# Attention weighing over a pair of units on eight 64x32 tiles, probabilities turned in place, six score buffers, tables laid out anew

## Time and profile before

| what | value |
|---|---|
| median of 3 runs | 2744.55 us |
| the runs | 2733.57, 2748.24, 2744.55 us |
| span of the profiled execution (first to last instruction) | 2740.3 us |
| TensorE busy, mean granted clock | 2332.0 us (85%), 0.951 of full speed |
| VectorE, ScalarE, GpSimd busy | 2165.5 (79%), 1538.2 (56%), 1436.9 us (52%) |
| image 5, from its norm0 to that of image 6 | 310.4 us |
| from the end of the last convolution to the end | 210.6 us |

### The profile page before, as it was taken

How to read it: one execution, slowest core, us unless ns; L and a number is a source line. 1 busy time by engine, 2 the same in 40 slices (tenths; PEclk the granted TensorE clock), 3 DMA queues, 4 the chain that set the end, 5 groups by cost and what they waited for, 6 DMA issues and landing times.

```text
span 2740.3 us, 67622 instructions
## 1 busy us (share of the span) xinstructions
PE 2332.0 (85%) x27766; PEld 1395.9 (51%) x27766; DVE 2165.5 (79%) x3697; ACT 1538.2 (56%) x3566; POOL 1436.9 (52%) x1150
## 2 busy tenths in 40 slices
PE   0457738899899989899898989899898999899887
PEld 0433326455654556554664556555664556545454
DVE  6877957878887798878887798869887788867655
ACT  1222126654775566754775566754766567655665
POOL 3324562456734574465834575465834575465455
PEclk9878969999999999999999999999999989999999
DMA  5400400115111331115111241105110241101121
GB/s 155 127 3 16 158 19 18 32 47 171 33 33 47 98 105 33 33 35 174 40 33 39 83 128 33 32 32 161 57 33 25 79 146 33 33 32 57 54 63 41
DMA packets 125428, 176.20 MB, mean 64 GB/s; under 512 B 72496, under 2 KB 114240, under 8 KB 115520
## 3 DMA queue, kind: packets, MB, share of 16 engines
q1 hardware_dynamic: 125120, 171.88, 20.0%
HBM read 98.95 MB, written 72.86 MB: 63 GB/s over the span
## 4 chain that ended last, share of the span: by engine, by line
PE 54%; DVE 23%; ACT 8%; issue 6%; POOL 4%; DMA 2%; SPq 2%; DVEq 0%; POOLq 0%; ACTq 0%
PE F L2082 18%; PE QP L2141 9%; PE QP L2148 4%; PE SP L2173 4%; PE F L1979 3%; PE O L2201 3%; PE QP L2157 3%; PE PTR L2183 2%; PE F L1955 2%; DVE g_raw L1423 2%; DVE xs L1836 2%; DVE mx L1847 1%; ACT xs L1201 1%; POOL tmp L960 1%; DVE sums L1855 1%
## 5 line engine op out<-in xcount | busy, mean ns | idle before, releaser
L2082 PE MATMUL F<-g_raw,cw_hi 128*128 128x512 f16 x2304 | 701.1, 386 | 20.7 <-DVE g_raw L1423 6.5
L1201 ACT ACTIVATE xs<-xs,mx 128x64 f32<-128x64 f32 x1792 | 445.7, 334 | 123.8 <-DVE mx L1847 123.8
L915 POOL TENSOR_TENSOR xs<-xs,rec 128x512 f32<-128x512 f32 x256 | 287.9, 1136 | 432.5 <-DVE rec L1857 428.3
L2082 PE MATMUL F<-g_raw,cw_lo 128*128 128x512 f16 x1152 | 443.8, 385 | 0.0
L2082 PEld LDWEIGHTS F<-g_raw,cw_hi 128*128 128x128 f16 x2304 | 224.2, 99 | 286.5 <-issue 17.8
L1208 ACT ACTIVATE prt<-PTR 128x512 f32<-128x512 f32 x256 | 151.0, 590 | 216.8 <-PE PTR L2183 191.0
L900 POOL TENSOR_TENSOR tmp<-X,uw 128x512 f32<-128x512 f32 x128 | 165.3, 1303 | 164.0 <-DVE y L1709 83.0
L1836 DVE TENSOR_TENSOR xs<-SP,bias 128x1024 f32<-128x1024 f32 (+2 forms) x192 | 159.7, 859 | 100.0 <-issue 54.2
L1423 DVE SCALAR_TENSOR_TENSOR g_raw<-l0c,gn,g_raw 128x512 f16<-128x512 f32 x192 | 171.6, 936 | 72.2 <-ACT g_raw L1140 36.9
L930 POOL TENSOR_TENSOR ot_lo<-ot,ot_hi 128x512 f16<-128x512 f32 x128 | 149.1, 1187 | 145.8 <-ACT ot_hi L1222 132.7
L2141 PE MATMUL QP<-tok_hi,qkv_hi 128*128 128x512 f16 x470 | 180.1, 383 | 43.4 <-ACT qq L1182 17.3
(11 more groups left out here) (331 smaller groups left out, 5586.4 us busy)
## 6 DMA issues: line engine op xcount, KB each, us to landing
scratch_x<-X SPq DMA_DIRECT2D x32, 1024.0 KB, 5.8
xs<-scratch_x SPq DMA_DIRECT2D x56, 508.0 KB, 3.4
out_x<-xs SPq DMA_DIRECT2D x56, 508.0 KB, 2.8
X<-in_x SPq DMA_DIRECT2D x25, 1024.0 KB, 6.3
l0c<-scratch_t SPq DMA_DIRECT2D x8, 1876.0 KB, 10.2
l0c<-in_x SPq DMA_DIRECT2D x7, 1024.0 KB, 6.5
l0c<-scratch_t SPq DMA_DIRECT2D x8, 640.0 KB, 12.8
l0c<-scratch_t SPq DMA_DIRECT2D x8, 576.0 KB, 13.7
```

The costliest lines, as they stand in the source:

```text
L915: G.tensor_tensor(keyed(sc[:, u % 4, :]), keyed(sc[:, u % 4, :]), rec[:, u % 4, :].unsqueeze(2).to_broadcast([P, 8, TOK]), ALU.mult).then_ ...
L1201: last = S.activation(keys, keys, ACT.Exp, bias=mx[:, u % 4, i:i + 1])
L2082: last = T.matmul(F[:, n % 2, :], wgt[:, ci, C3 * comp + dx, P * co:P * co + P], win[which], start=(ci == 0 and dx == 0 and j == 0), stop= ...
```

## The change

- One item W of TensorE is now the weighing of a pair of units (u, u+1): the same 32 calls on the same operands, with the loop over hs inside the loop over the four blocks b, so that 8 calls in a row go to eight different 64x32 tiles. It waits once, for both units' turned probabilities.
- `turned(u)` copies PTR back over the unit's own scores in `sc`; the buffers `prt` are gone, and with them its wait for the weighing of unit u-2.
- There are six buffers `sc` (`DEEP`), with six rows of `mx`, `sums` and `rec`. The bias addition of the pair (u, u+1) waits for `pv_done`, the weighing of the pair (u-6, u-5). The two new buffers lie where `prt` was, which the setup uses as scratch before.
- All tables of the order are new: FIRST, TURN, AHEAD and LAST_ROWS of all five queues. A TURN image has as many items of each stream as before, but 16 W for 32 on TensorE.

The tables for the streams that are spoken of, and the code (cut):

```diff
@@ FIRST["POOL"], its end (image 0) @@
-        "conv22.1": "W", "conv23.0": "WWWWRR", "conv23.1": "RRRRRRRRRRERRR", "convend": "RRRRRRRERRRRRR"},
+        "conv22.1": "W", "conv23.0": "W", "conv23.1": "WW", "convend": "WRRRRRRRRRRRRRRERRRRRRRR"},
...
@@ TURN["PE"] (images 1 to 7) @@
-    "PE": {"norm0b": "Q", "norm0c": "QT", "reduce0": "TQ", "reduce1": "QW", "reduce3": "Q", "reduce4": "T",
-        "reduce5": "QW", "reduce6": "SWT", "reduce7": "QS", "reduce8": "WQ", "reduce12": "Q", "reduce13": "T",
-        "reduce14": "Q", "reduce15": "Q", "hwconv": "QW", "hwgate": "TQTWQTWQW", "hwrows": "SQSQ", "band3": "Q",
-        "hwmean0": "Q", "hwmean3": "QTQ", "hwmean5": "Q", "hwmean6": "TW", "hwmean7": "TSWTW", "mix": "QWSQ",
-        "mixturn": "Q", "gate0": "T", "gate1": "Q", "gate3": "Q", "gate5": "QT", "gate6": "Q", "gate7": "TQ",
-        "gate8": "WSW", "gate9": "TSWW", "gate11": "Q", "gate12": "Q", "gate13": "Q", "gate16": "Q",
-        "gate17": "QQQT", "norm1a": "QT", "lift0": "SWT", "lift1": "WQ", "lift3": "STWWQ", "conv0.1": "Q",
-        "conv1.0": "Q", "conv2.1": "T", "conv6.1": "Q", "conv7.0": "Q", "conv7.1": "QT", "conv8.0": "Q",
-        "conv8.1": "WTWS", "conv9.1": "Q", "conv10.0": "T", "conv10.1": "SWW", "conv12.0": "Q", "conv12.1": "Q",
-        "conv13.1": "QT", "conv14.0": "Q", "conv15.0": "WQT", "conv15.1": "T", "conv16.0": "QT", "conv16.1": "WWQ",
-        "conv17.0": "QWS", "conv18.0": "S", "conv19.1": "Q", "conv22.1": "Q", "conv23.0": "Q",
-        "conv23.1": "TQTWWTQWQTEWE", "convend": "QEESEQSEQ"},
+    "PE": {"norm0c": "QQTQ", "reduce1": "Q", "reduce2": "T", "reduce3": "Q", "reduce4": "Q", "reduce5": "T",
+        "reduce6": "WST", "reduce7": "WSQ", "reduce8": "Q", "reduce11": "Q", "reduce13": "T", "reduce14": "QTQ",
+        "reduce15": "Q", "hwgate": "QTQTWQWS", "hwrows": "Q", "band0": "QS", "bandcopy": "Q", "hwmean1": "TQ",
+        "hwmean3": "Q", "hwmean4": "TQ", "hwmean6": "Q", "hwmean7": "TTS", "mix": "QWWSQ", "mixturn": "Q",
+        "gate1": "Q", "gate3": "Q", "gate4": "TQ", "gate6": "QT", "gate7": "Q", "gate8": "ST", "gate9": "TWSW",
+        "gate10": "Q", "gate12": "Q", "gate13": "QQ", "gate14": "T", "gate16": "QQ", "norm1a": "Q", "lift0": "TQ",
+        "lift1": "STWT", "lift2": "QWQ", "conv0.1": "Q", "conv1.1": "SQ", "conv2.1": "T", "conv5.0": "T",
+        "conv6.0": "Q", "conv6.1": "Q", "conv8.0": "Q", "conv8.1": "TQ", "conv9.0": "TSWW", "conv9.1": "Q",
+        "conv12.0": "S", "conv12.1": "TQ", "conv14.0": "Q", "conv14.1": "TQ", "conv15.0": "Q", "conv16.1": "Q",
+        "conv17.0": "TQ", "conv17.1": "Q", "conv18.0": "STQ", "conv19.0": "WSW", "conv20.1": "Q", "conv22.0": "Q",
+        "conv23.0": "Q", "conv23.1": "QTTQTWTQ", "convend": "EWEQEESQESEQ"},
...
-AHEAD = {"SP": {}, "POOL": {"R": 28, "E": 1, "N": 4, "O": 1}, "ACT": {"X": 2, "T": 4, "O": 1}, "DVE": {"U": 13, "E": 1, "T": 2, "A": 2}, "PE": {"Q": 2, "T": 4, "W": 4}}
+AHEAD = {"SP": {"L": 1}, "POOL": {"N": 4, "O": 1, "R": 22}, "ACT": {"O": 1, "T": 4, "X": 2}, "DVE": {"A": 4, "E": 1, "T": 2, "U": 7}, "PE": {"Q": 2, "T": 4, "W": 2}}
...
-    "PE": ("QQTQQQTQQWTSQTWSWWQQQQQQTTSWQQWTSTWWQQTQQQTQTWWSQTWWSQQQQTQQQTWSTTSWQWWQQQTQQQQTSTWWTQWWQSTQQWQQTQQW"
-            "TSWTSWQQQQQQQTQQTSTWWTSWWQQQQTQQTQWSTWTSWWQQTQQTWTWTWWQQ"),
+    "PE": ("QQTQQQTQTWSTQWSQQQQQQQTSTTSTWWQQQQTQTQQQQTSTQWWSQQQQTQTQQTSTWWSQQQQQQTQTSTWTSWQQQQTQQQTQTSTWWQQSQQQQ"
+          "QQTQSTQTWTWSQQQQQTQTSWTSTQWQTTQTWTQWQQ"),
...
-        xs = sb("xs", [P, (3 * CT + 4) * CHUNK])
+        xs = sb("xs", [P, (3 * CT + DEEP) * CHUNK])
         xr = xs[:, 0:3 * CT * CHUNK].rearrange("p (a t n) -> p a t n", a=3, t=CT)
-        sc = xs[:, 3 * CT * CHUNK:].rearrange("p (a n) -> p a n", a=4)
+        sc = xs[:, 3 * CT * CHUNK:].rearrange("p (a n) -> p a n", a=DEEP)
         coef = sb("coef", [P, 4, CT])
         c_alpha, c_beta, c_a3, c_b3 = (coef[:, i, :] for i in range(4))
-        prt = sb("prt", [P, 2, CHUNK])
-        mx = sb("mx", [P, 4, 8])
-        sums = sb("sums", [P, 4, 8])
-        rec = sb("rec", [P, 4, 8])
+        prt_flat = xs[:, (3 * CT + 4) * CHUNK:]
+        mx = sb("mx", [P, DEEP, 8])
+        sums = sb("sums", [P, DEEP, 8])
+        rec = sb("rec", [P, DEEP, 8])
...
                 def turned(u):
                     act.wait_ge(pt_done, u + 1)
-                    if u >= 2:
-                        act.wait_ge(pv_done, u - 1)
-                    S.activation(prt[:, u % 2, :], PTR[:, :], ACT.Copy).then_inc(pt_read, 1)
+                    S.activation(sc[:, u % DEEP, :], PTR[:, :], ACT.Copy).then_inc(pt_read, 1)
...
-                    r, quad, buf = u // 4, u // 2 % 2, u % 4
+                    r, quad, buf = u // 4, u // 2 % 2, u % DEEP
                     dve.wait_ge(s_done, u + 2)
-                    if u >= 4:
-                        dve.wait_ge(pt_done, u - 2)
+                    if u >= DEEP:
+                        dve.wait_ge(pv_done, u - DEEP + 2)
                     low = 2 * (r % NW == NW - 1)
...
                     for b in range(4):
-                        last = T.transpose(PTR[:, P * b:P * b + P], sc[:, u % 4, P * b:P * b + P], ident[:, :])
+                        last = T.transpose(PTR[:, P * b:P * b + P], sc[:, u % DEEP, P * b:P * b + P], ident[:, :])
                     last.then_inc(pt_done, 1)
 
                 def weigh(u):
-                    r, quad, hs = u // 4, u // 2 % 2, u % 2
-                    pe.wait_ge(pt_read, u + 1)
+                    r, quad = u // 4, u // 2 % 2
+                    pe.wait_ge(pt_read, u + 2)
                     if u % 4 == 0:
                         wait_read(pe, f"v1.{r}")
                         if r:
@@ -2193,16 +2191,17 @@
                     for b in range(4):
                         cg, wp = divmod(b, 2)
                         pair = 2 * quad + wp
-                        for h2 in range(2):
-                            h = 4 * cg + 2 * hs + h2
-                            for par in range(2):
-                                rows = slice(64 * par, 64 * par + 64)
-                                cols = 256 * cg + TOK * pair
-                                last = T.matmul(O[DH * (h % 4):DH * (h % 4) + DH, par, cols:cols + TOK],
-                                                vv[rows, pair, DH * h:DH * h + DH],
-                                                prt[rows, u % 2, P * b + TOK * h2:P * b + TOK * h2 + TOK],
-                                                start=True, stop=True)
-                    last.then_inc(pv_done, 1)
+                        cols = 256 * cg + TOK * pair
+                        for hs in range(2):
+                            for h2 in range(2):
+                                h = 4 * cg + 2 * hs + h2
+                                for par in range(2):
+                                    rows = slice(64 * par, 64 * par + 64)
+                                    last = T.matmul(O[DH * (h % 4):DH * (h % 4) + DH, par, cols:cols + TOK],
+                                                    vv[rows, pair, DH * h:DH * h + DH],
+                                                    sc[rows, (u + hs) % DEEP, P * b + TOK * h2:P * b + TOK * h2 + TOK],
+                                                    start=True, stop=True)
+                    last.then_inc(pv_done, 2)
 
                 def score_pairs():
                     for u in range(0, 4 * ROWS_ALL, 2):
@@ -2223,7 +2222,7 @@
                         yield u
 
                 def weighings():
-                    for u in range(4 * ROWS_ALL):
+                    for u in range(0, 4 * ROWS_ALL, 2):
                         weigh(u)
```

More of the change, by code:

```diff
@@ L37 @@
 GROUP = 8
+DEEP = 6
 HID = C // 16
@@ L1199, in exponential @@
                     for i in range(8):
-                        keys = sc[:, u % 4, TOK * i:TOK * i + TOK]
-                        last = S.activation(keys, keys, ACT.Exp, bias=mx[:, u % 4, i:i + 1])
+                        keys = sc[:, u % DEEP, TOK * i:TOK * i + TOK]
+                        last = S.activation(keys, keys, ACT.Exp, bias=mx[:, u % DEEP, i:i + 1])
                     last.then_inc(p_exp, 1)
```

31 lines of the change are left out of this document (14 added, 17 removed), and 111 rows, old and new, of tables (FIRST, TURN).

## The result

The changed kernel takes 2674.99 us (median of 4 runs, 2671.38 to 2680.29) against 2742.92 for the kernel before (median of 4). The ratio is 0.9757, 95% interval 0.9733 to 0.978: 68 us less. The forecast was 2693.0 with a range of 2660 to 2731. The profiled execution took 2680.29 us with a span of 2678.5, so it stands 5 us over the median; keep that in mind where spans are compared.

A forecast was written before the change was run, and what follows sets the result against it. TensorE was taken to bound half of each image and part of the rest. 2740.3 - 42 - 7 - 2 = 2689 us, plus 4 from span to median, gave 2693, range 2660 to 2731.

The forecast's parts named there:

- Step 1: TensorE's weighing: a pair on eight tiles takes 0.61 us, saving 7.6 us of TensorE's time in each of seven images.
- Step 2: Images 1 to 7: 6 of the 7.6 us of TensorE's time show per image, 42 us in all.
- Step 3: After the last convolution: 40 weighings as 20 pairs need 10.6 us less busy time; 7 us taken as gain.
- Step 4: ScalarE's copy of turned probabilities over their scores: costed at nothing, at most a gain of 24.7 us.
- Step 5: VectorE's bias addition waits for a weighing, 1.2 us later but of one pair earlier: cost 0, bounds -10 and 77.
- The rival that ends on the slower side: VectorE's bias addition: scores wait for late weighings, 1.2 us a pair, 2790 us if 80 are hit; chance 0.06.
- Step 6: Image 0's tables: six fewer GpSimd sums before image 1 save 2 us; moved setup letters cost 0, bounds -8 and +8.
- Step 7: mx, sums and rec of six rows and the scratch in xs: same instructions, 0 us.
- the tables fit better too: Images: with three pairs under way and fewer letters, idle time falls another 4 us an image, 2665 us; chance 0.14.
- eight tiles share their loads: Weighing: weight loads of eight tiles might queue in a steady run, leaving only the coupling's gain, 2724 us; chance 0.08.
- the signs of being wrong: A pair of 0.9 us or more; VectorE idle until a weighing; more idle TensorE in gate, reduce than weighing returned.

The follow-up runs named there:

- the pause: The changed kernel with two extra matmuls of 128x128 by 128 columns in the middle of each pair's weighing: 2725.77 us, ratio 0.9939.
- the code alone: The changed kernel with the old tables of the kernel before, the first W of each pair dropped: 2728.65 us, ratio 0.994.
- leaving three quarters out: The changed kernel with only the first eight of each pair's 32 weighing calls, after the first row: 2628.08 us, ratio 0.9578.
- the doubled one: The changed kernel with every pair's weighing done twice in a row: 2924.28 us, ratio 1.0674.
- the units in turn: The changed kernel with the loop over hs outermost in the weighing, one unit's four tiles after the other's: 2680.45 us, ratio 0.9764.

## Why the prediction was right, and where its steps were not

The total fell on the right side and within the range; the forecast was 18 us above what was measured. That the sum is so near is in part luck: two terms were off by some 20 us each, in opposite directions.

1. *Step 1, a pair on eight tiles*: that eight tiles work side by side was right, and the size was off. 0.61 us were set, 0.79 measured. The rate of 7 ns for eight tiles, read from 0.11 us of the old trace, held for the first 32 records and no longer. The sentence that failed is "what bounds a unit is its tiles, not the issue of instructions": it holds for four tiles at 14 ns, and for eight tiles from the 33rd record on something else bounds, by the pause and the late loads most likely the supply of instructions. The old row had the hint, as its stream fell back to 8 records in 0.11 us after 41; that was put down to four tiles at work alone. The gain by that step's own reckoning is 17.4 - 16 x 0.79 = 4.8 us of TensorE an image instead of 7.6. TensorE's busy time, drains included, fell by more: 6.7 us an image with the code alone (47 over seven) and 5.9 in the changed kernel (41.1 over seven).
2. *Step 2, how much shows*: 42 us were set; the two profiles have 23.9 in images 1 to 7, and the other profiles put it nearer 28. The code gives 18 on the old tables, and the new order the rest. 6 of 7.6 us is a share of 0.8; leaving three quarters out and the pause both give two thirds, and the code on the old tables gives 0.39. By stages of image 5, the stretch from `hwconv` on gave what was set (4.8 us for 4.6), `conv` less (1.2 for 2.1), and `gate` grew by 0.5 where it was to shrink.
3. *Step 3, last rows*: 7 were set and 10.8 measured, but the reason was another. The faster weighing gave nothing there with the old order (213.4 for 210.6); the new order gave 8.7 to 13.6, by which profile of it is taken. A row end waits for ScalarE and GpSimd, as the step itself said of some.
4. *Step 4, turned in place, at nothing*: held, ratio 0.9994.
5. *Step 5, the bias addition's new wait, at nothing*: held. It ended last in one place, 2.0 us. The rival that ends on the slower side never came up.
6. *Step 6, the tables of image 0, 2 us with bounds of -8 and +8*: this is the term that failed. 28.5 us were measured. The part that was priced, the six sums, was priced well (2 us in the trace, 3 to 4.5 in time). "The setup's letters are moved by a few steps; cost 0" was not read from rows: no window of image 0 stood in the argument. They show VectorE busy for 300 of 384 us and TensorE idle for half. Nor did it price what the AHEAD line showed beside the sums: six of VectorE's maxima (U at 7 for 13) leave image 0, and 9.6 us of VectorE's work with them.
7. *Step 7, nothing*: held.

By the two profiles, steps 1 and 2 gave 18 us too much, step 6 some 25 too little and step 3 some 4 too little; with the 5 us between profile and median that is the difference. With the other profiles of the same images, steps 1 and 2 gave some 14 too much, and most of the 5 us lies in the images. The rival "the tables fit better too" (2665) came nearer in number than the forecast, but not by its mechanism. TensorE's idle time in images 1 to 7 rose from 166.5 us to 183.6. It rose to 195.1 with the code alone, so the new order took back 11.5 of the 28.6 us, and made up for the code but no more. The rival "eight tiles share their loads" is refuted as it stood: loads and matmuls of eight tiles do run at 7 ns, 32 in a row, and again after a pause. Its doubt about a longer run was right all the same, and the loads are what comes late. Of the signs of being wrong only one came up, and that by 2.0 us: idle time of VectorE that a weighing ended. `gate` and `reduce` together have as much idle TensorE as before (7.0 us in image 5).

What stays open: which letters of the three engines in image 0 carry the 23 us, and what else in that table carries the other 5; how much of the rest belongs to the order of images 1 to 7; and what exactly ends the gaps of 1 to 2 us.

## What to carry to other kernels

Where a diff lays out tables anew, read the windows of every stretch that they order, the start of the kernel too; the edit that the change is named for may be the smaller part. A rate read from a tenth of a microsecond is shown for no longer: ask what feeds the stream. Small matmuls behind wide ones ran at full rate again here, so short dense streams may be better apart than one behind another; as a gain in time that was not tried. Measure how much of an engine's microsecond shows, by leaving some of its work out, and on the tables that you mean to keep: for TensorE it was two thirds on the new ones and 0.39 on the old, for VectorE a quarter. And read the granted clock beside each stretch before two profiles are compared.

## What the runs showed of the hardware

- **A dense stream of small matmuls slows after some 32 records.** After another kind of instruction, 32 records of 64x32 tiles on eight tiles begin in 0.238 us; after that most take 8 to 17 ns each. Two units on four tiles each, one after the other, keep their 14 ns a record in a stream of 64, but for the few that overlap at the change. Gaps come in besides: 17 of 0.4 to 1.9 us in the changed kernel's weighings (20.8 us), 75 of up to 5.5 us in the doubled one's (132 us), and 3 with the code alone on the old tables. 13 of the 14 with the units in turn stand at the same records as in the changed kernel. There are no rows for their cause; the doubled kernel moves 1.05 MB more in the queue that brings instructions.
- **The granted clock makes the same program differ from one execution to the next.** Images 1 to 7 of one and the same program took 2108.1 and 2121.8 us, with 66 and 97 us at the lower level of the clock and the same idle time of TensorE.
- **VectorE's instructions got slower with the tables.** Two groups, of the kernel before and of the changed one:

```profile
L1423 DVE SCALAR_TENSOR_TENSOR g_raw<-l0c,gn,g_raw 128x512 f16<-128x512 f32 x192 | 171.6, 936 | 72.2 <-ACT g_raw L1140 36.9 <-ACT g_raw L1062 35.2
L1821 DVE TENSOR_TENSOR tok_lo<-tok,tok_hi 128x512 f16<-128x512 f32 x128 | 94.2, 740 | 11.8 <-ACT tok_hi L1167 11.7
```

```profile
L1421 DVE SCALAR_TENSOR_TENSOR g_raw<-l0c,gn,g_raw 128x512 f16<-128x512 f32 x192 | 197.7, 1071 | 40.1 <-ACT g_raw L1062 35.2 <-ACT g_raw L1140 4.9
L1819 DVE TENSOR_TENSOR tok_lo<-tok,tok_hi 128x512 f16<-128x512 f32 x128 | 118.7, 932 | 20.2 <-ACT tok_hi L1167 19.8 <-PE QP L2155 0.2
```

With the new code on the old tables the two take 911 and 748 ns, so it is the order, not the code. Sorted by what GpSimd does meanwhile, the first group takes on average 748 ns in the changed kernel where GpSimd is idle or nearly so (103 of 192) and 1545 where it is busy throughout (54); before, these were 748 and 1529, but only 14 of 192 were of the second kind. The timeline has such a place, with GpSimd's instruction over VectorE's two:

```profile
495.30 2.35 POOL L814 TENSOR_TENSOR l0c<-l0c 128x1024 f32<-128x1024 f32 x1 [4.85 <-DVE l0c L1407]
496.08 2.79 DVE L1421 SCALAR_TENSOR_TENSOR g_raw<-l0c,gn,g_raw 128x512 f16<-128x512 f32 x2 [0.86 <-ACT g_raw L1062]
```

2.79 us for two that take 1.50 beside an idle GpSimd. The first of them ends 0.56 us after GpSimd's instruction does. The Trainium skill says in "SBUF — State Buffer", section "SBUF: two separate sides", that a VectorE operation with two SBUF inputs and a GpSimd operation that reads SBUF take turns on a pair of ports, one blocked for the whole of the other. The doubled durations agree with it. So a table can give part of its gain back: the two groups are 26.1 and 24.5 us longer in total, more than the 40 that VectorE's busy time grew in all.
